# Interleaving the two fc1 chunks and the two fc2 row blocks within a slot of TensorE

## The chip, the cores and the metric

The kernel runs on one core of a Trainium2 chip. The metric is device time in microseconds (us) of one execution. Before the change the median of three runs is 1412.71 us.

## The reference, cut to what matters

The input `x` has 16 batches of 512 rows with 512 columns, in fp32. Each batch goes through a conditioning step (attention pooling with a mask chosen by a type number of the batch) and then through a feed-forward network with dequantized weights; the input is added again at the end.

```python
attn_in = tanh(x @ W1 + b1);  scores = attn_in @ v              # cond
p = softmax(where(mask, scores, NEG_INF));  pooled = (p @ x) / cnt
h = (pooled - mu) * rsqrt(var + EPS) * ln_gamma + ln_beta        # ffn
y = silu(h @ w1 + fc1_bias)        # 512 x 2048, contraction over 512
z = y @ w2 + fc2_bias              # 512 x 512, contraction over 2048
out = x + pooled + 0.5 * z
```

## The kernel before, in words

Each engine runs its own instruction stream, written out by hand; semaphores join them. Work on a batch b is laid out in 32 slots (`ffn(b, p)`, one such function for PE, ACT and DVE). In the slots of batch b the kernel also runs steps of batch b+1 and b+2, so that the feed-forward network of one batch lies beside the conditioning of the next.

- **fc1** (`fc1`, L1087): the hidden layer has 16 tiles of 128 columns, and a tile is the sum of 4 chunks (c = 0 to 3) over the contraction. A slot does one chunk of two tiles, k ("tile A") and k+1 ("tile B"), each two matmuls of 128x512 (L1099, L1100). Between two chunks of a tile ACT multiplies the PSUM bank by a ratio (`rescale`, L590, some 0.62 us apart for the two); after the last chunk ACT does `silu` (L584). ACT takes A, then B, then the other steps of the slot, in that order. A chunk c > 0 waits for the rescale of the slot before; chunk 0 waits for the silu that frees its bank. `fc1_slot(i)` runs 5 slots ahead of the slot number: the first chunk of the next batch is in slot 27.
- **fc2** (`fc2`, L1116): hidden tile k = i // 2 is used in slots 2k and 2k+1, two row blocks in each, each three matmuls of 128x512 (L1124 to L1126). At row block 0, thus in even slots, PE waits for DVE's split of the tile (`split_y`, L886: y_hi at L891, y_lo at L893; in batch 0 ACT makes y_hi instead, L592, behind the rescales of its slot). DVE's splits are in its slots 0 and 3 of every 4.
- **Conditioning steps of PE** (`PE_PLAN`, L234), each at its slot: AT0 to AT3 in slots 30, 31, 0 and 1 (`project`, L1009 to L1011), SC in slot 2 (L1015), USUM and U in slot 9, DSUM in 11, PZ0 to PZ3 in slots 13 to 16 (`pool_block`, L1058 to L1063). In batch 0 the plan is 4 slots later. ACT loads another table and does the exponentials in slots 7 to 9 (`ACT_PLAN`, L237: L533, L541, L544).
- **SP's queue** (`turn`, L386): it waits for `xs_used`, which PE increments at L1060, the third matmul of a PZ step; after that of PZ3 (slot 16) it issues 16 DMAs of `load_columns` (L342), then, from batch 2 on, 16 DMAs of `move_h` (L384, behind `h_ready`), which carry the normalised rows to the partitions where DVE turns them (`TURNH`, L848, slot 24). ACT's `AFFINE` (L574, slot 25) and DVE's `SPLITH` (L858, L860, slot 26) follow, and the first chunk of the next batch in slot 27 waits for the last of these (`hT_done`).

```python
if k == 0:
    pe.wait_ge(hT_done, b * ND + (c + 1))
...
sp.wait_ge(xs_used, (b + 1) * NJ)
load_columns(b + 1)
if not by_pe(b):
    move_h(b)
```

Batches 2 to 13 run in a hardware loop of two batches for each pass; slot 0 of every even batch there is the start of a pass.

Of the kernel before, what the change touches and what calls it, by code (L numbers as in the profile page):

```python
# [18 lines left out]
def build(nc, x, itok, cond_w, cond_b, cond_v, gamma, beta, fc1_q, fc1_s, fc1_b, fc2_q, fc2_s, fc2_b, out):  # L19
# [20 lines left out]
    with ExitStack() as ctx:  # L40
# [229 lines left out]
        def cond_steps(b, i, steps, turn, moved):  # L270

            first = isinstance(b, int) and b == 0
            out = []
            if not (isinstance(b, int) and b == B - 1):
                out += [(1, name, n) for name, n in steps.get(i - DELAY if first else i, []) if first or i >= 0]
                out += [(1, name, n) for name, n in (turn if first else moved).get(i, [])]
            if not (isinstance(b, int) and b >= B - 2):
                out += [(2, name, n) for name, n in steps.get(i - SLOTS, [])]
            return out

        def fc1_slot(i):

            g, c = divmod(i + 5, ND)
            return g // NH, 2 * (g % NH), c

        def part_count(b, k, c):

            return b * PARTS + (k // 2) * 2 * (ND - 1) + c * 2 + k % 2 + 1

        def is_first(a):  # L290
            return isinstance(a, int) and a == 0

        def is_last(b):
            return isinstance(b, int) and b == B - 1
# [663 lines left out]
        def _(pe):  # L958
# [128 lines left out]
            def fc1(b, k, c):  # L1087

                if c == 0:
                    if k >= 2 or not is_first(b):  # L1090
                        pe.wait_ge(silu_done, b * NF + (k - 1))
                    if is_first(b) and k in w1_unit:
                        pe.wait_ge(w1_unit[k], 2)
                else:
                    pe.wait_ge(scaled, part_count(b, k, c - 1))
                if k == 0:
                    pe.wait_ge(hT_done, b * ND + (c + 1))
                o, w = y_ps[k % 2][:], w1[:, c, k * P:(k + 1) * P]
                mm(o, w, hT_hi[:, c, :], start=(c == 0), stop=False, skip_group_check=True)  # L1099
                last = mm(o, w, hT_lo[:, c, :], start=False, stop=True, skip_group_check=True)  # L1100
                last.then_inc(part_done if c < ND - 1 else fc1_done, 1)
# [14 lines left out]
            def fc2(b, k, r):  # L1116
                if r == 0:
                    if is_first(b) and k in w2_unit:
                        pe.wait_ge(w2_unit[k], 3)
                    pe.wait_ge(split_done, b * NF + (k + 1))  # L1120
                if k == 0 and not is_first(b):
                    pe.wait_ge(final_done, (b - 1) * NJ + (r + 1))
                rows = slice(r * P, (r + 1) * P)
                mm(z_ps[r][:], y_hi[k % 2][:, rows], w2_hi[:, k, :], start=(k == 0), stop=False)  # L1124
                mm(z_ps[r][:], y_hi[k % 2][:, rows], w2_lo[:, k, :], start=False, stop=False)  # L1125
                last = mm(z_ps[r][:], y_lo[k % 2][:, rows], w2_hi[:, k, :], start=False, stop=(k == NF - 1))  # L1126
                if r == NJ - 1:
                    last.then_inc(fc2_done, 1)
                elif k == NF - 1:
                    last.then_inc(z_rows, 1)  # L1130

            def ffn(b, p):
                for i in range(SLOTS):
                    ahead, k, c = fc1_slot(i)
                    if not (ahead and is_last(b)):
                        fc1(b + ahead, k, c)
                        fc1(b + ahead, k + 1, c)
                    for ahead, name, n in cond_steps(b, i, PE_PLAN, PE_TURN, {}):
                        steps[name](b + ahead, n, p if ahead == 2 else 1 - p)
                    for r in (2 * (i % 2), 2 * (i % 2) + 1):  # L1140
                        fc2(b, i // 2, r)

            pe.wait_ge(dve_const, 1)
            keep_busy_early(5)
# [32 lines left out]
            for k in (2, 3):  # L1177
                fc1(0, k, 0)
            ffn(0, 0)
            ffn(1, 1)  # L1180
            with pe.Fori(1, B // 2 - 1) as i:
                ffn(i * 2, 0)
                ffn(i * 2 + 1, 1)
# [27 lines left out]
```

## Time and profile before

| | |
|---|---|
| median of 3 runs | 1412.71 us (1410.33 to 1414.16) |
| the profiled execution | 1413.05 us |
| its span, first to last instruction | 1411.4 us |
| PE busy | 1365.8 us (97%) |
| DVE busy | 963.5 us (68%) |
| ACT busy | 895.3 us (63%) |
| mean granted TensorE clock | 0.990 |

The span is 1.65 us shorter than the execution's own time. PE's busy time counts matmuls whose modelled duration (390 ns) is longer than the distance at which they follow each other, so 97% says that there is nearly always one in flight, not that none is late. For the distance one has to read start times.

### The profile page before, as it was taken

The page shows a single profiled execution, that of the slowest core. Times are in us where ns is not written, and L with a number is a line of the kernel's source. Part 1 is how long each engine was busy: PE and PEld are TensorE (multiplying, and loading weights), DVE is VectorE, ACT ScalarE, POOL GpSimd, SP SyncE. Part 2 cuts the span into 40 slices and gives each one's busy share as a digit, 9 for nine tenths or more (in the row PEclk, how much of TensorE's full clock was granted, in tenths as well). Part 3 has the DMA queues.
Part 4 walks back from the last instruction along what each step waited for, and adds up shares of the span by engine and source line. Part 5 has one row for each costly group of instructions (what it writes and reads, how often), then busy time and mean ns, then how long its engine had stood idle before and what let it go on. Part 6 is the DMA issues. An engine that isn't in the chain of part 4 may idle for free.

```text
span 1411.4 us, 21112 instructions
## 1 busy us (share of the span) xinstructions
PE 1365.8 (97%) x6235; PEld 1076.7 (76%) x6235; DVE 963.5 (68%) x1922; ACT 895.3 (63%) x1422; POOL 197.9 (14%) x156
## 2 busy tenths in 40 slices
PE   7878999999999999999999999999999999999999
PEld 5656777787777878777787777878777787877887
DVE  7579676758666685776758667675876668677522
ACT  3557666656666666666666666665666666666654
POOL 5022111011110111111011110101111011111100
PEclk9799999999999999999999999999999999999999
DMA  9631203131130313203131230313113031220100
GB/s 296 167 119 24 66 1 61 60 60 61 27 78 17 60 60 50 71 4 56 60 60 61 32 87 0 60 61 56 63 20 75 26 60 60 44 76 1 30 31 30
DMA packets 271377, 82.28 MB, mean 58 GB/s; under 512 B 247514, under 2 KB 248116, under 8 KB 270772
## 3 DMA queue, kind: packets, MB, share of 16 engines
q1 hardware_dynamic: 271152, 81.31, 24.1%
q14 instruction: 73, 0.60, 0.2%
q8 instruction: 20, 0.33, 0.1%
q10 hardware_dynamic: 132, 0.05, 0.0%
HBM read 49.86 MB, written 16.78 MB: 47 GB/s over the span
## 4 chain that ended last, share of the span: by engine, by line
PE 64%; SPq 15%; issue 7%; DVE 7%; ACT 4%; DMA 2%; DVEq 0%; ACTq 0%
PE y_ps L1099 12%; PE z_ps L1124 11%; PE y_ps L1100 11%; PE z_ps L1126 11%; PE z_ps L1125 11%; SPq L384 9%; SPq L342 6%; DMA h_cols<-scratch 2%; ACT y_f L584 1%; ACT y_ps L590 1%; PE a_ps L1058 1%; PE a_ps L1060 1%; PE a_ps L1059 1%; PE a_ps L1015 1%; PE a_ps L1026 1%
## 5 line engine op out<-in xcount | busy, mean ns | idle before, releaser
L590 ACT ACTIVATE y_ps<-y_ps,ratio 128x512 f32<-128x512 f32 x768 | 474.2, 655 | 332.8 <-PE y_ps L1100 330.8
L1099 PE MATMUL y_ps<-hT_hi,w 128*128 128x512 f32 x1016 | 405.7, 399 | 17.7 <-DVE w L872 8.7
L1124 PE MATMUL z_ps<-w_hi,y_hi 128*128 128x512 f32 x1024 | 409.9, 400 | 1.3 <-DVE y_lo L893 1.1
L1125 PE MATMUL z_ps<-w_lo,y_hi 128*128 128x512 f32 x1024 | 399.9, 390 | 0.0
L1126 PE MATMUL z_ps<-w_hi,y_lo 128*128 128x512 f32 x1024 | 399.8, 390 | 0.0
L1100 PE MATMUL y_ps<-hT_lo,w 128*128 128x512 f32 x1016 | 397.7, 391 | 0.0
L891 DVE CAST y_hi<-y_f 128x512 fp32r<-128x512 f32 x240 | 115.6, 482 | 261.6 <-ACT y_f L584 161.2
L1099 PEld LDWEIGHTS y_ps<-hT_hi,w 128*128 128x128 f32 x1016 | 191.3, 188 | 82.3 <-ACT y_ps L590 21.5
L584 ACT ACTIVATE y_f<-y_ps,vec_cols,mant 128x512 f32<-128x512 f32 x256 | 185.1, 774 | 87.7 <-PE y_ps L1100 87.7
L1124 PEld LDWEIGHTS z_ps<-w_hi,y_hi 128*128 128x128 f32 x1024 | 192.8, 188 | 60.9 <-issue 19.6
L1125 PEld LDWEIGHTS z_ps<-w_lo,y_hi 128*128 128x128 f32 x1024 | 192.9, 188 | 42.3 <-issue 3.6
L1126 PEld LDWEIGHTS z_ps<-w_hi,y_lo 128*128 128x128 f32 x1024 | 192.7, 188 | 40.7
L1100 PEld LDWEIGHTS y_ps<-hT_lo,w 128*128 128x128 f32 x1016 | 191.9, 189 | 36.9
L893 DVE TENSOR_TENSOR y_lo<-y_f,y_hi 128x512 fp32r<-128x512 f32 x256 | 192.6, 753 | 32.7 <-ACT y_hi L501 24.4
L434 POOL TENSOR_TENSOR x<-x,scratch 128x512 f32<-128x512 f32 x64 | 87.0, 1362 | 667.8 <-ACT scratch L562 667.8
L442 POOL TENSOR_TENSOR x<-x,b2h 128x512 f32<-128x512 f32 x64 | 99.3, 1581 | 459.1 <-DVE hT_lo L860 410.8
L821 DVE BATCH_NORM_STATS2 stats<-scratch 128x6 f32<-128x512 f32 x64 | 44.2, 690 | 41.9 <-ACT scratch L562 41.8
L848 DVE STREAM_TRANSPOSE h_rows<-h_cols 128x512 f32<-128x512 f32 x56 | 34.9, 680 | 32.4 <-DMA h_cols<-scratch 32.4
L562 ACT ACTIVATE scratch<-a_ps,columns 128x512 f32<-128x512 f32 x64 | 44.1, 690 | 10.6 <-PE a_ps L1063 4.3
L574 ACT ACTIVATE h_rows<-h_rows,vec_cols 128x512 f32<-128x512 f32 x56 | 42.5, 809 | 4.5 <-DVE h_rows L848 4.0
L739 DVE TENSOR_TENSOR xs_lo<-x,xs_hi 128x512 fp32r<-128x512 f32 x60 | 41.5, 692 | 2.1
L901 DVE TENSOR_TENSOR x<-z_ps,x 128x512 f32<-128x512 f32 x64 | 40.9, 677 | 2.2 <-PE z_ps L1126 2.2
(194 smaller groups left out, 1117.5 us busy)
## 6 DMA issues: line engine op xcount, KB each, us to landing
x<-in_x_dram SPq DMA_DIRECT2D x64, 256.0 KB, 3.7
out_dram<-x SPq DMA_DIRECT2D x64, 256.0 KB, 2.1
x_cols<-in_x_dram SPq DMA_DIRECT2D x240, 64.0 KB, 2.1
h_cols<-scratch SPq DMA_DIRECT2D x224, 64.0 KB, 2.1
fc_codes<-in_L_ffn_fc_q_dram SPq DMA_DIRECT2D x8, 1024.0 KB, 12.5
e<-in_L_ffn_fc_scales_dram SPq DMA_DIRECT2D x4, 1024.0 KB, 12.2
fc_scaled<-in_L_ffn_fc_scales_dram SPq DMA_DIRECT2D x4, 1024.0 KB, 15.8
scratch<-in_L_cond_W_dram SPq DMA_DIRECT2D x1, 256.0 KB, 3.5
```

The source lines that it names most:

```text
L384: sp.dma_start(h_cols[piece, :, i * Q:(i + 1) * Q], rows[i * Q:(i + 1) * Q, :, piece]).then_inc(h_moved, 16)
L434: nc.gpsimd.tensor_tensor(xt[p][:, J, :], xt[p][:, J, :], pooled[J], ALU.add).then_inc(res_added, 1)
L442: nc.gpsimd.tensor_tensor(xt[p][:, J, :], xt[p][:, J, :], b2h[:], ALU.add).then_inc(bias_added, 1)
L584: nc.scalar.activation(y_f[k % 2][:], y_ps[k % 2][:], ACT.Silu, bias=b1[:, k:k + 1], scale=mant[:, (ND - 1) * NF + k:(ND - 1) * NF + k + 1 ...
L590: nc.scalar.activation(y_ps[k % 2][:], y_ps[k % 2][:], ACT.Copy, scale=ratio[:, c * NF + k:c * NF + k + 1]).then_inc(scaled, 1)
L891: v.tensor_copy(y_hi[k % 2][:], y_f[k % 2][:]).then_inc(yhi_done, 1)
L893: v.tensor_tensor(y_lo[k % 2][:], y_f[k % 2][:], f32(y_hi[k % 2][:]), ALU.subtract).then_inc(split_done, 1)
L1099: mm(o, w, hT_hi[:, c, :], start=(c == 0), stop=False, skip_group_check=True)
L1100: last = mm(o, w, hT_lo[:, c, :], start=False, stop=True, skip_group_check=True)
L1124: mm(z_ps[r][:], y_hi[k % 2][:, rows], w2_hi[:, k, :], start=(k == 0), stop=False)
L1125: mm(z_ps[r][:], y_hi[k % 2][:, rows], w2_lo[:, k, :], start=False, stop=False)
L1126: last = mm(z_ps[r][:], y_lo[k % 2][:, rows], w2_hi[:, k, :], start=False, stop=(k == NF - 1))
```

## The change

Before, PE did in each slot: chunk of tile A, chunk of tile B, conditioning step, fc2 row block, fc2 row block. After: chunk of tile A, one fc2 row block, chunk of tile B, conditioning step, the other fc2 row block. No instruction is added or removed, and the waits stay with their instructions: the one of fc2 on the split moves ahead of tile B's chunk and of the conditioning step. The streams of ACT, DVE, POOL and SP aren't touched.

```diff
             def ffn(b, p):
                 for i in range(SLOTS):
                     ahead, k, c = fc1_slot(i)
-                    if not (ahead and is_last(b)):
+                    runs_fc1 = not (ahead and is_last(b))
+                    if runs_fc1:
                         fc1(b + ahead, k, c)
+                    fc2(b, i // 2, 2 * (i % 2))
+                    if runs_fc1:
                         fc1(b + ahead, k + 1, c)
                     for ahead, name, n in cond_steps(b, i, PE_PLAN, PE_TURN, {}):
                         steps[name](b + ahead, n, p if ahead == 2 else 1 - p)
-                    for r in (2 * (i % 2), 2 * (i % 2) + 1):
-                        fc2(b, i // 2, r)
+                    fc2(b, i // 2, 2 * (i % 2) + 1)
```

## Rows read from the trace of the kernel before

**Rows 1.** The page: busy times, chain that ended last by engine, PE's loads.

```profile
PE 1365.8 (97%) x6235; PEld 1076.7 (76%) x6235; DVE 963.5 (68%) x1922; ACT 895.3 (63%) x1422; POOL 197.9 (14%) x156
...
PE 64%; SPq 15%; issue 7%; DVE 7%; ACT 4%; DMA 2%; DVEq 0%; ACTq 0%
...
L1125 PEld LDWEIGHTS z_ps<-w_lo,y_hi 128*128 128x128 f32 x1024 | 192.9, 188 | 42.3 <-issue 3.6
```

**Rows 2.** Waits of the whole span: who for whom, total us, times, longest.

```profile
SPq L342 <- PE a_ps L1060: 587.8, 15, 51.4
...
DVE h_rows L848 <- DMA h_cols<-scratch: 32.4, 14, 2.9
...
PE a_ps L1009 <- DVE u_rows L732: 7.1, 5, 1.6
PE y_ps L1099 <- ACT y_f L584: 7.0, 16, 1.1
```

**Rows 3.** Chain that ended last, 632 to 658 us: start, us, what.

```profile
632.37 0.24 PE a_ps L1060
632.78 0.34 SPq L342
...
641.65 0.62 SPq L384
...
651.73 2.08 DMA h_cols<-scratch
...
657.50 0.47 PE y_ps L1099
```

**Rows 4.** Timeline of PE, slot 7: start, us, engine, line; second row tile B's last.

```profile
605.29 0.39 PE L1099 MATMUL y_ps<-hT_hi,w 128*128 128x512 f32 x1
...
605.97 0.39 PE L1100 MATMUL y_ps<-hT_lo,w 128*128 128x512 f32 x1
...
607.55 0.39 PE L1099 MATMUL y_ps<-hT_hi,w 128*128 128x512 f32 x1
```

**Rows 5.** Timeline of ACT, slots 7 and 8.

```profile
605.94 1.24 ACT L590 ACTIVATE y_ps<-y_ps,ratio 128x512 f32<-128x512 f32 x2 [0.81 <-PE y_ps L1100]
607.20 1.28 ACT L533 ACT_TABLE_LOAD   x1
...
609.20 1.21 ACT L590 ACTIVATE y_ps<-y_ps,ratio 128x512 f32<-128x512 f32 x2
```

**Rows 6.** Timeline of PE, start of slot 9, tile A's chunk.

```profile
609.88 0.50 PE L1099 MATMUL y_ps<-hT_hi,w 128*128 128x512 f32 x1
610.22 0.40 PE L1100 MATMUL y_ps<-hT_lo,w 128*128 128x512 f32 x1
```

**Rows 7.** Timeline, slot 1 at the start of a pass: PE, then DVE.

```profile
588.89 0.39 PE L1100 MATMUL y_ps<-hT_lo,w 128*128 128x512 f32 x1
590.88 0.50 PE L1009 MATMUL a_ps<-coef,wc_hi 128*128 128x512 f32 x1 [1.60 <-DVE u_rows L732]
...
590.14 0.68 DVE L732 TENSOR_TENSOR u_rows<-scratch,coef 128x512 fp32r<-128x512 f32 x1
```

**Rows 8.** Timeline of PE, slot 30, tile B's chunk.

```profile
665.15 0.50 PE L1099 MATMUL y_ps<-hT_hi,w 128*128 128x512 f32 x1
665.48 0.39 PE L1100 MATMUL y_ps<-hT_lo,w 128*128 128x512 f32 x1
```

**Rows 9.** Timeline of batch 0 around the start of slot 8: ACT, DVE, PE.

```profile
82.37 0.63 ACT L501 ACTIVATE y_hi<-y_f 128x512 fp32r<-128x512 f32 x1
...
83.14 0.69 DVE L893 TENSOR_TENSOR y_lo<-y_f,y_hi 128x512 fp32r<-128x512 f32 x1 [3.29 <-ACT y_hi L501]
...
83.98 0.47 PE L1124 MATMUL z_ps<-w_hi,y_hi 128*128 128x512 f32 x1
```

**Rows 10.** Batch 0, slot 11: timeline of PE; window: us, busy (x) by engine, PEclk.

```profile
98.68 0.77 PE L1099 MATMUL y_ps<-hT_hi,w 128*128 128x512 f32 x1 [7.11 <-DVE w L872]
...
98.60:102.60 4.00, 3.92 (x10) 3.17 (x11) 2.77 (x4) 2.48 (x4) 0.00 (x0) 0.57 0.00 0
```

## The prediction

> **What bounds the kernel now.** I read the busy times first, then the chain that ended last, then the waits, then the timelines at the places they point to. PE is busy for 97% of the span, but only 64% of the chain lies on it: 15% is SP's queue [rows 1]. That can't be if PE alone sets the end. A quiet slot of PE shows its pace: the first matmul of one slot starts at 605.29, that of the next at 607.55, ten matmuls in 2.26 us, so 0.226 us each [rows 4]. In such a slot nothing can be gained by an order, as nothing waits.
>
> The chain between 632 and 658 us shows the other bound. It leaves PE at L1060 (632.37, PZ3 in slot 16), and SP starts its 16 `load_columns` at 632.78. The 16 `move_h` follow without a hole from 641.65, the last starts at 651.73 and has landed 2.08 us later, DVE turns, and PE's first chunk of the next batch, slot 27, starts at 657.50 [rows 3]. So from L1060 to slot 27 there are 25.13 us that PE can't shorten by working faster, while its ten slots in between take less. SP waits for that L1060 each time, 587.8 us in 15 waits: it is never late by itself [rows 2]. The arrival at slot 27 costs PE an idle wait in nearly every batch, 16 waits on L1099 with 7.0 us in total [rows 2]. They are booked to ACT's silu; in the row of 657.50 the chain behind it leads through SP's queue and the DMA. A batch therefore takes (slot 27 to L1060 of the next slot 16, on PE) plus (the 25.13 us chain). Time that PE loses or wins in slots 27 to 16 counts in full; in slots 17 to 26 it doesn't.
>
> **The change part by part.** Nothing is removed; three matmuls (one row block) go ahead of tile B's chunk and of the conditioning step.
>
> 1. *Every conditioning step of PE is 3 x 0.226 = 0.68 us later in its slot.* For most, the consumer is late by the same amount and meets PE again in a conditioning step that has moved too, so it costs nothing. One consumer meets PE in something that hasn't moved: L1060 of PZ3 starts SP's 32 DMAs, and these end at tile A's chunk in slot 27, which is first in its slot before and after. Queued behind are `load_columns`, `move_h`, DVE's turn, ACT's affine and silu, all in order. Since the DMAs follow one another without a hole [rows 3], nothing in the chain absorbs the shift. It is paid once for each batch that `move_h` serves, 2 to 15: 14 x 0.68 = +9.5 us. DVE's turn waits for the DMA exactly 14 times, 32.4 us in all [rows 2], so the DMA is what comes last there. Bounds: 0 if the chain had 0.68 us of slack, which the wait at 657.50 speaks against, and 9.5.
>
> 2. *ACT gets tile B 0.68 us later.* A rescale starts 0.42 us after its L1100 has started (605.52 by the pace, 605.94 on ACT), two take 1.24 us [rows 4, 5]. B's L1100 starts at 605.97, so it was ready for ACT at 606.39 and ACT took it at about 606.56, 0.17 us later. After the change it is ready at 607.07: ACT's queue is late by 0.68 - 0.17 = 0.51 us behind it. Mostly ACT idles after that (0.81 us before the pair in this row), so that's free. Not in slots 7 and 8: the table load, the exponentials and the rescales follow without a hole, 607.20 to 609.20 and on [rows 5], and slot 9 starts on PE at 609.88, just when A's rescale (609.20 + 0.62) is done [rows 6]. It will start at about 610.39: +0.51. Inside slot 9 B's pair follows at once now instead of 0.34 us apart, the mark of a chunk whose wait was still open (A's shows it in [rows 6]): -0.11. Net +0.40, in slots that count, 14 times: +5.6 us. Bounds 0 and 0.51 each.
>
> 3. *B has three matmuls more of cover.* In slot 30 its pair is 0.33 us apart instead of 0.226 [rows 8]; that goes: -0.11 x 14 = -1.5 us. At the start of a pass of the loop PE waits at AT3 in slot 1: L1100 at 588.89, then L1009 only at 590.88, because DVE's u_rows starts at 590.14 [rows 7]. There are 5 such waits, 7.1 us [rows 2]. DVE doesn't hang on PE's order there (its ACT input may come up to 0.25 us later by part 2). AT3 starts at the same time, but only three matmuls of the slot come behind it instead of six: each wait shrinks by 0.45 to 0.68, I take 0.5: -2.5 us. What is late next is SP's chain; these slots lie in the part that counts.
>
> 4. *The wait of fc2 on the split now has B's chunk and the conditioning step queued behind it.* In batches 1 to 15 DVE makes both halves a slot or so early, so it costs nothing; if that margin were gone each would cost B's cover. In batch 0 it is not free. y_hi is made by ACT behind the rescales (82.37), y_lo by DVE at 83.14, and PE's L1124 of slot 8 starts at 83.98, 0.15 us after y_lo ends [rows 9]: already the last thing to arrive. Now ACT is 0.51 us later (part 2), so L1124 at 84.49, and B's two matmuls (0.45), which used to be done in the meantime, come behind it: +0.96 us in that slot. Slots 4, 8, 12, ..., 28 are built alike, seven of them: 7 x 0.96 = 6.7. Some are absorbed: in slot 11 PE waits 7.11 us for DVE's weights [rows 10], and only the delay of DVE gets through there. In others a conditioning step is queued behind too. I take +6; bounds 2 and 10.
>
> A rule of the Trainium skill would price each moved matmul otherwise. Rows: a weight load lasts 188 ns [rows 1], and yet matmuls with their own weights follow at 0.226 us [rows 4], so the load of the next lies under the running one. "TensorE: Matmul & The Clock Gate", section "Part 3: Packing small matmuls", says that a weight load overlaps running matmuls only when its row group differs, and all these use all rows. By that rule a moved matmul would weigh 0.188 more, the shift 1.24 instead of 0.68, and part 1 some 7.9 us more. The trace doesn't agree with it, so the sum goes by the rows.
>
> Sum: +9.5 + 5.6 - 1.5 - 2.5 + 6 = +17.1 us, on the profiled execution of 1413.05 us: 1430.2. That execution is 0.34 us above the median, so nothing is corrected. Forecast 1430.
>
> **The rivals.**
>
> - *Only ACT and batch 0 count* (part 1 is hidden by slack in the chain): 1413 + 5.6 - 1.5 - 2.5 + 6 = 1420.6. For it: the wait in slot 27 is booked to silu. Against: that silu stands behind the affine steps, and they behind the DMA. Chance 0.09.
> - *Colder clock.* The seven holes of batch 0 grow; after the long one in slot 11 (7.11 us) the granted clock is 0.57 over the next 4 us, so mostly the lower level, 1.2 of 2.4 GHz, and the first matmul lasts 0.77 instead of 0.39 us [rows 4, 10]. If the clock falls there once or twice more, a slot or two at half pace, 2.3 us each, is added: about 1435. Chance 0.10.
> - *Faster:* if slot 27 is truly set by ACT's silu pair and PE, not by SP, and ACT's queue swallows the 0.51 us, then the cover is what counts: AT3 5 x 0.68, the pairs in slots 9 and 30, 0.11 each in 15 batches, together -6.7, so about 1406. It decides from the point where the last DMA of `move_h` lands 0.68 us before DVE is free to turn. Against: DVE idles before each of the 14 turns [rows 2]. Chance 0.04.
> - *No effect:* the gains and the startup's losses cancel, 1413. The instructions are reordered as written, so the change does what it says; this needs parts 1 and 2 both wrong. Chance 0.05.
>
> **How the numbers follow.** Forecast 0.72, colder clock 0.10, ACT and batch 0 only 0.09, no effect 0.05, faster 0.04. The range of 8 in 10 takes the forecast's bounds (batch 0 at 2 or 10, slot 9 a third less) and the next case on each side: 1420 to 1438. A measurement of this kernel can tell about 0.3% from no change, 4.2 us. Faster by more: 0.04; within: 0.05; slower by more: 0.91.
>
> **What would show it.** In a middle batch, L1060 of PZ3 to the first L1099 of slot 27 is still about 25.1 us, and the period of two batches grows by 2 x 0.97 us where no pass starts, less 0.5 where one does. PE's wait on L1099 in slot 27 is 0.68 us longer, some 9 us more in the list of waits. SP's L342 starts 0.4 us after L1060, later in its slot. Slot 9 starts half a us late; ACT's table load there stands 0.5 us later. The waits at AT3 shrink to about 1.0 us. In batch 0, L1124 waits for y_lo at nearly every fourth slot. The forecast is wrong if the 25.13 us shrink (slack was there), if DVE's y_lo is late in middle batches (then it is worse), or if batch 0 takes up its delays in the weights' waits.

## The result and the profile after

The changed kernel takes 1436.05 us (median of 4, 1435.96 to 1436.42) against 1413.22 us for the kernel before in the same comparison: ratio 1.0166, 95% interval 1.0148 to 1.0183, 22.8 us slower. The profiled execution took 1435.96 us with a span of 1434.4 us. Forecast was 1430, with a range of 1420 to 1438.

The page: busy times, and the chain that ended last by engine.

```profile
PE 1367.5 (95%) x6235; PEld 1079.0 (75%) x6235; DVE 972.8 (68%) x1922; ACT 938.2 (65%) x1422; POOL 201.1 (14%) x156
...
PE 62%; SPq 13%; issue 8%; DVE 7%; ACT 6%; DMA 2%; ACTq 0%; DVEq 0%
```

PE is busy for as long as before to within 2 us [rows 1]: the work is the same, and 21 of the 23 us are idle time of PE. The waits say where (engine and line, whom it waited for, total us, times, longest):

```profile
DVE h_rows L848 <- DMA h_cols<-scratch: 41.7, 14, 3.9
...
PE y_ps L1099 <- ACT y_f L584: 16.3, 16, 2.0
PE y_ps L1099 <- ACT y_ps L590: 11.0, 18, 2.0
...
PE a_ps L1009 <- DVE u_rows L732: 5.6, 5, 1.2
PE z_ps L1124 <- DVE y_lo L893: 5.3, 6, 1.7
...
PE z_ps L1124 <- DVE w_lo L882: 2.0, 1, 2.0
```

The 16 waits booked to silu, 14 of them in slot 27 and two in the start-up, hold 16.3 us instead of 7.0, the DMA is waited for 9.3 us longer, and AT3's 5 waits shrink from 7.1 to 5.6 [rows 2]. The waits on ACT's rescale were 2 with 2.0 us before: of the 16 new ones 14 are in slot 9 of batches 1 to 14 and two in batch 0. The six waits on y_lo, where there was one of 1.1 us, are all in batch 0.

In a middle batch the chain looks as before. SP's queue, and PE around slot 16 and at slot 27 (timeline: start, us, what):

```profile
648.44 0.39 PE L1060 MATMUL a_ps<-xs_hi,part_lo 128*128 128x512 f32 x1
...
649.02 8.74 SPq L342 DMA_DIRECT2D x_cols<-in_x_dram  x16
657.91 10.72 SPq L384 DMA_DIRECT2D h_cols<-scratch  x16
```

The chain that ended last, same stretch:

```profile
667.99 2.08 DMA h_cols<-scratch
670.09 0.72 DVE h_rows L848
...
673.77 0.47 PE y_ps L1099
```

From SP's first issue to slot 27 it is 673.77 - 649.02 = 24.75 us; before it was 657.50 - 632.78 = 24.72 [rows 3]. The chain kept its length and started later in the batch: L1060 follows the first matmul of slot 16 after 2.04 us (648.44 - 646.40) instead of 1.36. To compare whole stretches I laid the starts of tile A's chunk side by side, slot by slot, in both traces. In a middle batch only these slots have another length: slot 26, at whose end PE waits for the chain (+0.25 to +0.93, most often +0.68, 9.3 us in all), slot 8, which ends with the wait of slot 9 (+0.56 each time, 7.8 us in all), slot 9 itself (-0.10 to -0.13, 1.6 in all), slot 30 (-0.10 to -0.14, 1.5 in all), and slot 1 at the start of a pass (-0.04 to -0.53, 1.4 in all). Four passes of the loop, two batches each, take 170.08 us each instead of 168.19. Batch 0 (from its slot 0 to the start of the next batch) lost 10.9 us, and all that follows 12.8; the stretch ahead of slot 0 was 0.7 us shorter in this trace, which makes up the 23.0 us between the two spans.

### The profile page after: what moved, and what is told of

Its sections match the earlier page's. It is cut to its first block, busy times and chain, and to the rows that moved or that the text cites. A ratio compares the mean times of both kernels' runs of the same rounds, so it can differ in the third digit from the quotient of the medians.

```text
span 1434.4 us, 21112 instructions
## 1 busy us (share of the span) xinstructions
PE 1367.5 (95%) x6235; PEld 1079.0 (75%) x6235; DVE 972.8 (68%) x1922; ACT 938.2 (65%) x1422; POOL 201.1 (14%) x156
## 4 chain that ended last, share of the span: by engine, by line
PE 62%; SPq 13%; issue 8%; DVE 7%; ACT 6%; DMA 2%; ACTq 0%; DVEq 0%
PE y_ps L1099 11%; PE z_ps L1124 11%; PE y_ps L1100 11%; PE z_ps L1125 10%; PE z_ps L1126 10%; SPq L384 8%; SPq L342 5%; DMA h_cols<-scratch 2%; ACT y_ps L590 1%; ACT L533 1%; ACT y_f L584 1%; DVE x L901 1%; PE a_ps L1015 1%; PE a_ps L1060 1%; PE a_ps L1059 1%
## 5 line engine op out<-in xcount | busy, mean ns | idle before, releaser
L590 ACT ACTIVATE y_ps<-y_ps,ratio 128x512 f32<-128x512 f32 x768 | 503.4, 660 | 331.7 <-PE y_ps L1100 329.4
L1099 PE MATMUL y_ps<-hT_hi,w 128*128 128x512 f32 x1016 | 402.8, 396 | 35.8 <-ACT y_f L584 16.3
L1124 PE MATMUL z_ps<-w_hi,y_hi 128*128 128x512 f32 x1024 | 410.9, 401 | 7.3 <-DVE y_lo L893 5.3
L891 DVE CAST y_hi<-y_f 128x512 fp32r<-128x512 f32 x240 | 108.9, 454 | 225.9 <-ACT y_f L584 144.6
L1124 PEld LDWEIGHTS z_ps<-w_hi,y_hi 128*128 128x128 f32 x1024 | 193.0, 189 | 69.5 <-issue 24.3
L584 ACT ACTIVATE y_f<-y_ps,vec_cols,mant 128x512 f32<-128x512 f32 x256 | 197.3, 778 | 71.4 <-PE y_ps L1100 71.2
L893 DVE TENSOR_TENSOR y_lo<-y_f,y_hi 128x512 fp32r<-128x512 f32 x256 | 207.0, 808 | 43.1 <-ACT y_hi L501 30.6
L434 POOL TENSOR_TENSOR x<-x,scratch 128x512 f32<-128x512 f32 x64 | 91.0, 1423 | 682.8 <-ACT scratch L562 682.8
```

The lines of the kernel that those rows point to most:

```text
L434: nc.gpsimd.tensor_tensor(xt[p][:, J, :], xt[p][:, J, :], pooled[J], ALU.add).then_inc(res_added, 1)
L584: nc.scalar.activation(y_f[k % 2][:], y_ps[k % 2][:], ACT.Silu, bias=b1[:, k:k + 1], scale=mant[:, (ND - 1) * NF + k:(ND - 1) * NF + k + 1 ...
L590: nc.scalar.activation(y_ps[k % 2][:], y_ps[k % 2][:], ACT.Copy, scale=ratio[:, c * NF + k:c * NF + k + 1]).then_inc(scaled, 1)
L891: v.tensor_copy(y_hi[k % 2][:], y_f[k % 2][:]).then_inc(yhi_done, 1)
L893: v.tensor_tensor(y_lo[k % 2][:], y_f[k % 2][:], f32(y_hi[k % 2][:]), ALU.subtract).then_inc(split_done, 1)
```

## The experiments

Each kernel was timed against the kernel before on the same chip. The medians of before differ a little from one comparison to the next (1411.6 to 1412.3 us), and the intervals of the ratios reach 1.5 to 4 us to either side, so the tenths of a difference say little. The numbers per slot come from the profiled execution of each kernel, slot by slot against that of before.

**Slot 16 alone.** `split` chooses the order of the change in a slot, otherwise the order of before:

```diff
+                    split = not is_first(b) and i == 16
```

> The order of the change in slot 16 alone (where PZ3 releases SP), in batches 1 to 15; all else as before. Theory (SP's chain has no slack): PZ3's third matmul comes 0.68 us later, SP's 32 DMAs and slot 27 follow, 14 x 0.68 = +9.5 us, 1422.7 us. Rival (the chain has slack, slot 27 is set by ACT's silu): +0, 1413.2 us.

1422.47 us against 1412.12, ratio 1.0066 (1.0040 to 1.0091): +10.4 us. One slot in 32, with three matmuls in another place and nothing more. Its waits:

```profile
DVE h_rows L848 <- DMA h_cols<-scratch: 42.5, 14, 3.9
PE y_ps L1099 <- ACT y_f L584: 17.0, 16, 2.0
```

The waits booked to silu are 17.0 us, 10.0 more than in [rows 2]. The rival, that the chain has slack, is out. That it is SP's part of the chain this run alone doesn't show, since ACT and DVE too get what PE does in slot 16 later; the edit on SP further down does. Of the profiled execution's loss 1.5 us belong to a single stretch of lower clock in batch 2, which isn't the edit's regular price.

**Slot 7 alone.**

```diff
+                    split = not is_first(b) and i == 7
```

> The order of the change in slot 7 alone, in batches 1 to 15. Theory (ACT takes tile B 0.51 us later and has no hole until slot 9): slot 9 starts 0.51 to 0.56 us later, 14 times, +7.1 to +7.8 us, 1420.7 us. Rival (ACT's idle time takes it up, or what PE loses here comes back before SP's chain): +0, 1413.2 us.

1420.65 us, ratio 1.0059 (1.0040 to 1.0078): +8.5 us. Slot 9 starts 0.56 us later, and in the waits it stands as

```profile
PE y_ps L1099 <- ACT y_ps L590: 8.5, 16, 1.3
PE y_ps L1099 <- ACT y_f L584: 8.0, 16, 1.2
```

These are 16 waits on the rescale where there were 2 with 2.0 us, the 14 new ones in slot 9, and the waits booked to silu are nearly unchanged at 8.0.

**Batch 0 alone.**

```diff
+                    split = is_first(b)
```

> The order of the change in batch 0 alone. Theory (what the start-up lost in the changed kernel is its own, since ACT makes y_hi and PE queues tile B's chunk and the conditioning step behind it): the changed kernel was 10.2 us behind at the end of batch 0, so +10.2 us, 1423.4 us. Rival (part of it is made up later, where slot 27 waits for SP's chain anyway): +4 to +7 us.

1423.41 us, ratio 1.0075 (1.0054 to 1.0096): +11.3 us. In the trace batch 0 lost 10.7 us, and the later batches made up nothing of it.

**All the rest.**

```diff
+                    split = not is_first(b) and i not in (7, 16)
```

> The change everywhere except batch 0 and slots 7 and 16 of the others. Theory (the loss sits in these three places alone and the rest is gain by tile B's cover): 14 x (-0.12 in slot 9, -0.11 in slot 30) and 5 x -0.52 at AT3, together -5.7 us, 1407.5 us. Rival (the loss is spread over all slots, as each fc2 now stands ahead of a chunk): slower than 1413.2, towards 1420 us.

1407.19 us, ratio 0.9967 (0.9955 to 0.9979): 4.9 us faster than before. The four parts (+10.4, +8.5, +11.3, -4.9) sum to 25.3 us for 22.8 measured, within what four medians can be off; by the ratios they sum to 1.67% for 1.66%. The order as such is a small gain; three places turn it into a loss.

**Slots 17 to 26 alone.**

```diff
+                    split = not is_first(b) and 17 <= i <= 26
```

> The order of the change in slots 17 to 26 alone, in batches 1 to 15, where PE does fc1 and fc2 and no conditioning step while SP's chain runs. Theory (time on PE doesn't count here, and the order costs nothing where ACT has a hole): no change, 1412.1 us. Rival (putting a row block between the chunks costs PE something in every slot): 10 slots in 15 batches, +0.05 us in each would be +7.5 us.

1412.31 us against 1411.79, ratio 1.0005 (0.9994 to 1.0015): no change: the interval leaves room for 2.1 us and not for the rival's 7.5. Ten slots per batch with the order of the change cost nothing that can be measured.

**SP's queue cut open, in both kernels.** The buffers of `x_cols` 0 and 2 lie where PZ2 has read last, so half of the loads needn't wait for PZ3 (`load_columns` takes the numbers of the buffers as an argument here):

```diff
-                sp.wait_ge(xs_used, (b + 1) * NJ)
-                load_columns(b + 1)
+                sp.wait_ge(xs_used, (b + 1) * NJ - 1)
+                load_columns(b + 1, (0, 2))
+                sp.wait_ge(xs_used, (b + 1) * NJ)
+                load_columns(b + 1, (1, 3))
```

On the kernel before:

> The kernel before with one edit on SP: the 8 loads of x_cols 0 and 2, whose buffers PZ2 frees, go out one slot earlier, the other 8 after PZ3. Theory (SP's queue between PZ3 and slot 27 sets the batch): move_h can start when h_ready comes, which was 0.46 to 1.15 us earlier than SP's turn in 13 batches, 7.0 us in all beyond the 0.12 us that a released issue takes; -7 us, 1405 us. Rival (slot 27 is set by ACT's silu or DVE's work, not by SP): 1412 us.

1404.93 us against 1411.55, ratio 0.9945 (0.9923 to 0.9967): 6.6 us faster. Its waits (lines are two further down here):

```profile
DVE h_rows L850 <- DMA h_cols<-scratch: 25.1, 14, 2.5
...
PE y_ps L1101 <- ACT y_f L586: 1.3, 3, 0.6
```

The waits booked to silu went from 7.0 us in 16 to 1.3 in 3, of which one is in slot 27, although no instruction of ACT was touched: it was SP. The waits of SP's queue show what comes last in the chain instead:

```profile
SPq L384 <- DVE scratch L843: 82.2, 14, 48.9
```

Before, `move_h` waited for DVE's normalised rows once; now it does so 14 times. In a middle batch SP's loads end at 631.14 and DVE's rows at 633.95, and `move_h` starts at 633.98.

On the changed kernel:

> The same edit on SP in the changed kernel, where SP's turn came 0.80 to 2.04 us after h_ready. Theory: 12.2 us of the 23 come back, 1424 us; what stays is slot 9 and batch 0. Rival: no gain, 1436 us.

1422.43 us, ratio to before 1.0066 (1.0043 to 1.0089): 13.6 us of the 22.8 come back, the theory said 12.2 (between the profiled executions it is 11.8). With this edit two batches take 168.64 us instead of 170.08.

**Both gains together**: the order of "All the rest" with the early loads.

> The change without batch 0 and slots 7 and 16, with the early loads of SP. Theory: both gains add, since they lie in different stretches of the batch: 1407.2 - 6.3 = 1401 us. Rival (with SP out of the way another engine sets slot 27, and the cover gained elsewhere is given back): 1405 to 1407 us.

1403.68 us, ratio 0.9935 (0.9910 to 0.9959). The rival is nearer: of the 4.9 us that the order gained alone, 1.3 are left beside the SP edit (1403.68 to 1404.93, less than these runs can tell apart). Two batches take 167.06 us, with SP's edit alone 167.29. The order's gains lie between slot 27 and slot 16, where PE hands over to SP. The two traces show where most of them are given back: against SP's edit alone, slot 27 is longer by 0.2 to 0.35 us in most batches, 2.8 us in all, and slot 26 by 0.9 us in all. In one of these batches ACT idles 0.47 us for slot 25's tile B, which comes later in the new order; the affine and silu steps stand behind it in ACT's queue, and slot 28 starts 0.05 us after ACT's rescale. That this path is the cause was not tested. This is the fastest version found, 7.9 us below before, and most of it, 6.6 us, is SP's edit.

**ACT's order in slot 7**, on the changed kernel: the table load and first exponential go between the two rescales.

```diff
                         for t in (k, k + 1):
+                            if t == k + 1 and i == 7 and not is_first(b) and not is_last(b):
+                                steps["EXPE"](b + 1, 0)
...
+                        if name == "EXPE" and not is_first(b):
+                            continue
```

> The changed kernel; in slot 7 of batches 1 to 14 ACT does the table load and the first exponential between the rescales of tile A and tile B, thus in the hole that waiting for B left. Theory (slot 9 is late since ACT stood idle for B): 14 x 0.5 us come back, 1429 us. Rival (slot 9 is late for another reason, or tile B's rescale is now too late for slot 8): 1436 us or more.

1427.91 us, ratio to before 1.0102 (1.0075 to 1.0129): 8.1 us back of the 22.8. In the trace slot 8 is 0.11 us longer than before instead of 0.56, and slot 9 shorter by 0.24 instead of 0.11. ACT in slots 7 and 8, first in the changed kernel, then with this edit:

```profile
622.22 0.66 ACT L590 ACTIVATE y_ps<-y_ps,ratio 128x512 f32<-128x512 f32 x1 [0.47 <-PE y_ps L1100]
622.90 1.28 ACT L533 ACT_TABLE_LOAD   x1
...
624.90 1.21 ACT L590 ACTIVATE y_ps<-y_ps,ratio 128x512 f32<-128x512 f32 x2
```

```profile
616.37 0.66 ACT L590 ACTIVATE y_ps<-y_ps,ratio 128x512 f32<-128x512 f32 x1 [0.35 <-PE y_ps L1104]
617.05 1.28 ACT L533 ACT_TABLE_LOAD   x1
618.34 0.22 ACT L533 ACTIVATE e_all<-columns 128x12 f32<-128x12 f32 x1
618.46 0.64 ACT L590 ACTIVATE y_ps<-y_ps,ratio 128x512 f32<-128x512 f32 x1
```

In the first, tile B's rescale stands alone behind an idle 0.47 us, where before the two were one piece without a hole [rows 5]. In the second ACT works through the hole, and tile B's rescale at 618.46 is still in time. The waits on the rescale fall from 11.0 us in 18 to 3.2 in 3, none of them in slot 9.

**Batch 0, three cuts.** All with the order of the change in batch 0 only, to be compared with the 1423.41 us of "Batch 0 alone". Without the slots in which fc2 waits for the split:

```diff
+                    split = is_first(b) and i % 4 != 0
```

> The order of the change in batch 0 alone, without slots 0, 4, 8, ..., 28, where fc2 waits for the split. Theory (the larger part of batch 0's loss is what stands behind that wait, tile B's chunk and the conditioning step): of 11.3 us about 3.5 stay, from ACT being 0.5 us late at seven places, 1415.6 us. Rival (the loss comes from ACT taking B, and y_hi behind it, later): 1421 to 1423 us.

1417.14 us against 1411.79, ratio 1.0037 (1.0025 to 1.0049): +5.4 us instead of +11.3. Theory and rival stood at 3.5 and about 10. The queue behind the wait is the larger part, as the theory had it. The rest isn't all ACT's delay: in the trace 2.2 us lie in slot 24, which lost nothing with the full change. PE waits there for DVE's normalised rows, and the lower clock follows (timeline of PE, then a window: us, busy (x) of PE, PEld, DVE, ACT and POOL, granted clock, DMA share, GB/s):

```profile
143.44 1.86 PE L1078 MATMUL a_ps<-ident,scratch 128*128 128x128 f32 x8 [2.36 <-DVE scratch L841]
...
143.60:147.00 3.40, 3.40 (x13) 3.01 (x13) 1.51 (x3) 0.78 (x1) 0.00 (x0) 0.50 0.00 0
```

The full change has three such stretches in slots 4 to 31 that the kernel before hasn't, and this cut has one, so the cut also changed where the clock fell.

Without slot 4:

```diff
+                    split = is_first(b) and i != 4
```

> The order of the change in batch 0 alone, without slot 4. Theory: in slot 4 PE waits for w_lo (DVE, L882), not only for y_lo, and tile B's chunk and AT2 stand behind it, 3.2 us of batch 0's 11.3; DVE's weights in slot 11 are late by less, so nearly all of it comes back: 1423.3 - 3 = 1420 us. Rival (slot 11, where PE waits for DVE's weights anyway, takes slot 4's loss up): no gain, 1423 us.

1418.46 us, ratio 1.0043 (1.0029 to 1.0058), +6.1 us: slot 4 alone is worth some 5.

Without slot 28:

```diff
+                    split = is_first(b) and i != 28
```

> The order of the change in batch 0 alone, without slot 28. Theory: the late y_lo in slot 28 holds back tile B's chunk, with it ACT's rescale and y_hi, DVE's SPLITH and TURN, and through ACT's XT0 the chunk of slot 30: 3.3 us, all of which come back: 1420 us. Rival (DVE is late there for its own work, from the slots before): only slot 28's 1.0 us, 1422.3 us.

1418.71 us, ratio 1.0047 (1.0029 to 1.0065), +6.4 us: slot 28 is worth some 5 too. In the traces, counted from slot 0 to the start of the next batch, the saving is 4.2 us for each, but it isn't all theirs. Without slot 4, 2.7 us come back in slot 4 and 1.6 in slot 30. Without slot 28, only 2.8 us come back in slots 28 to 30 (0.5, 0.7 and 1.6); the other 1.4 are in slot 0, whose instructions are the same in both: at its start the granted clock was 1.00 in this run and 0.54 in "Batch 0 alone". The 1.6 us in slot 30 are clock in both cases. In the changed kernel, slots 4 and 30 of batch 0 (timeline of PE, then windows, with the columns as above):

```profile
71.01 0.39 PE L1100 MATMUL y_ps<-hT_lo,w 128*128 128x512 f32 x1
73.45 0.61 PE L1124 MATMUL z_ps<-w_hi,y_hi 128*128 128x512 f32 x1 [2.05 <-DVE w_lo L882]
...
168.92 0.52 PE L1099 MATMUL y_ps<-hT_hi,w 128*128 128x512 f32 x1 [2.05 <-ACT y_ps L590]
...
73.40:77.00 3.60, 3.55 (x9) 2.77 (x10) 0.00 (x0) 1.20 (x3) 0.00 (x0) 0.54 0.00 0
...
168.80:172.80 4.00, 3.88 (x10) 3.05 (x11) 3.61 (x6) 2.64 (x5) 4.00 (x3) 0.57 0.01 4
```

Without slot 4, the wait in slot 30 is there as long as ever, but the clock stays up behind it:

```profile
165.46 0.50 PE L1099 MATMUL y_ps<-hT_hi,w 128*128 128x512 f32 x1 [2.07 <-ACT y_ps L590]
...
165.40:169.40 4.00, 3.94 (x17) 3.29 (x18) 3.60 (x6) 2.79 (x6) 4.00 (x3) 1.00 0.02 4
```

Slot 30 is 1.47 us longer than before in the changed kernel, and 0.13 us shorter here: the same wait of 2.05 to 2.07 us costs 1.60 us more when 1.2 GHz is granted behind it than when 2.4 is.

Slot 4 has such a pair too. The kernel with ACT's order changed does the same as the changed kernel in batch 0, and PE waits as long in slot 4 (lines are four further down), but the clock stays up:

```profile
72.46 0.50 PE L1128 MATMUL z_ps<-w_hi,y_hi 128*128 128x512 f32 x1 [2.05 <-DVE w_lo L886]
...
72.40:76.00 3.60, 3.54 (x15) 2.92 (x16) 0.74 (x3) 1.98 (x4) 0.00 (x0) 1.00 0.00 0
```

Slot 4 is 1.69 us longer than before there, and 3.28 in the changed kernel: again 1.6 us are clock.

## Why the prediction was right, and where its sizes were off

**The bound** (SP's chain between PZ3 and slot 27): shown by four runs. Three matmuls ahead of PZ3 in slot 16 cost their full time; ten slots behind it with the same order cost nothing; half of SP's loads earlier gives 6.6 us to the old kernel and 13.6 to the new.

**Step 1**, +9.5 us by 14 x 0.68: 10.4 measured alone, 9.3 in the trace of the changed kernel. The 14th arrival, that of batch 15, didn't shift (-0.04): there are no loads for a batch 16 ahead of its `move_h`, which waits for DVE's rows. The other 13 give 0.25 to 0.93 each, 0.67 to 0.71 in batches 3, 5, 7, ..., 13, and mostly more in the others. The rival that named ACT's silu (1420.6) had only the booking of the wait for it, and the edit on SP emptied these waits.

**Step 2**, ACT 0.51 us late in slot 7, net +5.6 us: 0.56 in the trace where slot 7 alone gave +8.5 us (7.1 expected); the reordered ACT gave 8.1 back. The size was a tenth low. Net of what slot 9 gives back it is 7.8 - 1.6 = 6.2 us in the trace. Nearly all of the 0.56 is there when ACT starts the table load, 622.90 - 620.43 = 2.47 us after the first matmul of slot 7 instead of 607.20 - 605.29 = 1.91 [rows 4, 5]: 0.51 as forecast for the start of tile B's rescale, and the rescale by itself lasts 0.66 us, where the sum had 0.62 for one of a pair.

**Step 3**, -1.5 and -2.5 us: slot 30 gave the 1.5. AT3 gave 1.4 and not 2.5, since its five waits shrank from 1.15 to 1.60 us to 1.05 to 1.24 and not by the 0.5 taken for each. With slot 9's 1.6 that makes 4.5 us of gains in the trace of the changed kernel, and 4.9 were measured in the run that kept only the gains. This is part of why two batches grew by 1.89 us, where 2 x 0.97 less 0.5 = 1.44 was forecast.

**Step 4** is the term that was mis-sized: +6 us forecast for batch 0, 10.9 in the trace and 11.3 in the run, above its bound of 10. Three things are in it. First, slot 4 was priced like the others at 0.96 us. It lost 3.28. Before, PE reached fc2 there when w_lo was nearly done:

```profile
72.96 0.50 PE L1124 MATMUL z_ps<-w_hi,y_hi 128*128 128x512 f32 x1 [0.17 <-DVE w_lo L882]
```

Now L1124 comes 0.55 us later in its slot (73.45 - 70.79 against 72.96 - 70.85), and behind it stand not only tile B's two matmuls but AT2's three, 5 x 0.227 = 1.1 us. The prediction named this case ("a conditioning step is queued behind too") and gave it no number. The rest of slot 4, some 1.6 us, is half-rate clock: its eleven matmuls take 4.2 us from 73.45 on, and 2.6 (72.46 to 75.09) at full clock in the kernel with ACT's order changed. Second, slot 28 was not the end of its own loss: the trace shows 1.03 us in slot 28 and 0.74 in slot 29, where PE's wait before slot 30 is 2.05 us instead of 1.32. The late chunk of tile B holds back ACT's rescale and y_hi, these DVE's y_lo, SPLITH and TURN, and ACT's XT0, which waits for TURN, stands ahead of the rescale that slot 30 needs. Leaving out slot 28 removed the 0.74 and half of the 1.03. Third, the colder clock, which stood as a rival of 0.10 at 1435, did occur, at slot 4, at slot 30 and once between, in slot 19. The first two cost 1.6 us each, 3.2 of the 4.9 us by which step 4 was short; slots 18 and 19 together lost 0.9, and how much of that is clock was not taken apart. I had taken it as an alternative; it was an addition to the forecast's own case. The remaining losses are smaller and spread: 1.60 in slot 8, 1.04 in slot 1, and 0.5 to 0.8 in slots 11, 12, 16 and 21; slots 20 and 24, priced at 0.96, lost nothing.

**The sum in the terms of the trace**: 9.3 + 6.2 - 1.5 - 1.4 + 10.9 = 23.5 us, less 0.7 for the shorter stretch ahead of slot 0, is 22.8; the spans differ by 23.0. The mechanisms of all four steps were right. The time came out 6 us above the forecast, mostly by step 4. With batch 0 at its own bound of 10 the sum is 1434.2; that 1436 lies well inside the stated range is owed to the next case, the colder clock, for which the range was drawn up to 1438.

Absorption in slot 11 was right in kind: the changed kernel was 4.8 us behind at the start of slot 10 and 4.0 at the start of slot 11, which is when DVE's weights are there.

**A matmul's weight** of 0.68 for three: L1060 comes 2.04 - 1.36 = 0.68 us later in slot 16, with all three loads under running matmuls. The rule that the prediction quotes from the Trainium skill ("TensorE: Matmul & The Clock Gate", section "Part 3: Packing small matmuls"), that a weight load overlaps running matmuls only when its row group differs, would have made it 1.24. The trace decides against the rule for these loads.

**Open** stays what sets the clock's falls in batch 0, and with them part of what each slot there costs. Once SP's loads are early, `move_h` waits for DVE's rows, and PE has one wait left in slot 27; whether PE's own slots or DVE then bound the batch no run took apart. That two runs of batch 0 save 5 us by the medians and 4.2 in the traces is within what such medians differ by.

## What to carry to other kernels

Before work is moved within an in-order queue, look for what the moved instructions release, not only for what they wait for: three matmuls ahead of a semaphore that started 32 DMAs cost 10 us, and the same three in ten other slots cost nothing. A wait that moves forward should be priced with everything that is now behind it, and with the clock that may fall during it. And a wait booked to the engine that came last (here silu) can be settled cheaply by starting the suspected transfer earlier.

## What the runs showed of the hardware that was not expected

Two waits of PE of the same length at the same place, 2.05 and 2.07 us, left the granted clock at 0.57 over the next 4 us in one kernel and at 1.00 in the other. The half-rate stretch cost 1.60 us. In slot 4 two kernels whose batch 0 has the same instructions waited 2.05 us each, and the clock over the next 3.6 us was 0.54 in one and 1.00 in the other. Whether the lower clock follows such a wait can't be read from the wait's length; in batch 0 of the changed kernel it did in slots 4 and 30. So a cut that moves these waits can gain or lose 1.6 us that have nothing to do with what was cut.
